# Attention followed by a state-space layer on one core: the convolution's first group projected in step 10 instead of 11, and the state's product behind the value matmuls of its step

## The reference

```python
# layer 0: attention over all 4096 pixels of an image
energy = q @ k                       # q, k: 32 channels
x1 = gamma * (softmax(energy) @ v) + x
# layer 1: on x1, per pixel in order
u = layernorm(x1)
z, xBC, dt = split(u @ in_w)         # 256, 512 and 4 columns
xBC = silu(causal_conv4(xBC) + b)    # 4 taps per channel
xs, Bm, Cm = split(xBC)              # 256, 128, 128
state = state * exp(dt*A) + (dt * xs) outer Bm
y = (state @ Cm + D * xs) * silu(z)
out = rmsnorm(y) @ out_w
result = x1 + out * sigmoid(mlp(mean(out)))
```

## Time and profile before

| | |
|---|---|
| median of 3 runs | 3118.52 us (3118.3 to 3119.95) |
| the profiled execution | 3119.77 us, span of its core 3117.6 us |
| PE busy | 2935.3 us, 94% |
| DVE, ACT, POOL busy | 66%, 62%, 64% |
| mean granted clock of PE | 0.978 |

### The profile page before, as it was taken

One profiled execution on the slowest core, in us unless ns is written; L12 is line 12 of the kernel. 1 busy time (PEld: TensorE's weight loads), 2 busy tenths in 40 slices (PEclk: granted clock), 3 DMA queues, 4 the chain that ended last, 5 costly groups with the idle time before them and its releaser, 6 DMA issues. The chain is left out here.

```text
span 3117.6 us, 62448 instructions
## 1 busy us (share of the span) xinstructions
PE 2935.3 (94%) x20696; PEld 2263.6 (73%) x20696; DVE 2047.6 (66%) x3577; ACT 1924.6 (62%) x3806; POOL 1991.1 (64%) x3087
## 2 busy tenths in 40 slices
PE   6889999999999999999999999999999999999974
PEld 3767777777767777777777777777777777777752
DVE  5556666666767666666676667676666667776553
ACT  2555666666656666666665666666666666666642
POOL 2446665677666676666676666576777666777753
PEclk9999999999999999999999999999999999999985
DMA  4111111111312112122221122122120111111021
GB/s 124 49 43 34 45 58 58 32 55 52 97 68 65 63 60 92 65 78 75 93 81 37 65 71 87 65 73 86 38 90 36 50 63 50 63 50 70 35 95 68
DMA packets 102512, 200.94 MB, mean 64 GB/s; under 512 B 18768, under 2 KB 41936, under 8 KB 97808
## 3 DMA queue, kind: packets, MB, share of 16 engines
q1 hardware_dynamic: 98192, 195.08, 18.4%
q10 hardware_dynamic: 4000, 1.86, 0.2%
HBM read 131.21 MB, written 64.75 MB: 63 GB/s over the span
## 5 line engine op out<-in xcount | busy, mean ns | idle before, releaser
L724 POOL TENSOR_TENSOR p_lo<-p,p_hi 128x512 f16<-128x512 f32 x1024 | 1201.4, 1181 | 747.7 <-ACT p_hi L887 598.5
L880 ACT ACTIVATE p<-p_et 128x512 f32<-128x512 f32 x1024 | 614.3, 600 | 603.3 <-PE p_et L1138 556.8
L1156 PE MATMUL acc<-v_hi,p_hi 128*128 128x257 f16 x4096 | 954.1, 273 | 2.6 <-DVE work L1456 1.5
L1158 PE MATMUL acc<-v_lo,p_hi 128*128 128x256 f16 x4096 | 952.2, 272 | 0.0
L1412 DVE TENSOR_REDUCE maxes<-p_mx 128x1 f32<-128x1024 f32 x508 | 619.8, 1220 | 321.2 <-PE p_mx L1117 321.1
L887 ACT ACTIVATE p_hi<-p 128x512 f16<-128x512 f32 x1024 | 646.2, 631 | 8.3
L1164 PE MATMUL acc<-v_hi,p_lo 128*128 128x257 f16 x4096 | 623.3, 274 | 16.4 <-POOL p_lo L724 16.4
L1156 PEld LDWEIGHTS acc<-v_hi,p_hi 128*128 128x128 f16 x4096 | 399.4, 98 | 128.8 <-issue 65.8
L1158 PEld LDWEIGHTS acc<-v_lo,p_hi 128*128 128x128 f16 x4096 | 400.5, 98 | 112.3 <-issue 43.3
L1164 PEld LDWEIGHTS acc<-v_hi,p_lo 128*128 128x128 f16 x4096 | 400.0, 98 | 69.9 <-POOL p_lo L724 17.6
L1138 PE MATMUL p_et<-qs,kst 98*128 98x256 f16 x2048 | 393.1, 273 | 3.6 <-ACT p L880 2.9
(11 more groups left out here) (214 smaller groups left out, 4160.3 us busy)
## 6 DMA issues: line engine op xcount, KB each, us to landing
work<-rows_d SPq DMA_DIRECT2D x32, 1024.0 KB, 4.9
xin<-in_x_dram SPq DMA_DIRECT2D x48, 512.0 KB, 5.0
xr<-in_x_dram SPq DMA_DIRECT2D x32, 512.0 KB, 3.7
x_d<-x1c SPq DMA_DIRECT2D x31, 512.0 KB, 3.0
og_d<-og SPq DMA_DIRECT2D x29, 512.0 KB, 2.7
mix_x<-x_d SPq DMA_DIRECT2D x25, 512.0 KB, 4.6
mix_o<-og_d SPq DMA_DIRECT2D x24, 512.0 KB, 5.5
out_dram<-mix_o SPq DMA_DIRECT2D x24, 512.0 KB, 3.0
```

The costliest lines, as they stand in the source:

```text
L724: e.tensor_tensor(p_lo[:, n % RING, :], p32[:, n % P32S, :], p_hi[:, n % RING, :], ALU.subtract).then_inc(lo_pool, 1)
L880: e.activation(p32[:, n % P32S, :], p_et[:, :], ACT.Exp).then_inc(exp_done, 1)
L1156: e.matmul(acc[:, t, 0:C + 1], p_hi[:, r, at:at + P], v_hi[:, 2 * k + kk, 0:C + 1], start=(k == 0 and kk == 0), stop=False)
L1158: e.matmul(acc[:, t, 0:C], p_hi[:, r, at:at + P], v_lo[:, 2 * k + kk, :], start=False, stop=False, skip_group_check=True)
```

## The change

Two things. `K_XBC[0]` goes from 11 to 10, which moves the first convolution group, with everything that follows it by a fixed number of steps, one step earlier on PE, ACT and DVE (in the last group all four). And `st` is no longer issued directly behind `y`, but behind `values` of the same step on PE; DVE's addition to the state (L1578) moves from the step of `y` to the one after it. No instruction is added or removed, and no DMA moves.

```diff
--- before.py
+++ after.py
@@ -49,7 +49,7 @@
 
 K_X1T, K_UT, K_DT, K_DAT, K_CUM, K_YT, K_OUT = 3, 9, 15, 25, 27, 30, 0
 K_U = (6, 7)
-K_XBC = (11, 16, 20, 26)
+K_XBC = (10, 16, 20, 26)
 K_Z = (10, 11, 13, 15)
 K_XSB = (26, 27, 28, 29)
 K_SRC = (1, 5, 9, 13)
@@ -143,7 +143,7 @@
             if K == K_CB[c]:
                 out += [("cb", Bk, c)]
             if K == K_Y[c]:
-                out += [("y", Bk, c), ("st", Bk, c)]
+                out += [("y", Bk, c)]
         if K == K_YT:
             out += [("yT", Bk, 0), ("yT", Bk, 1)]
     if s < G:
@@ -162,6 +162,9 @@
             out += [("se1", b, 0)]
         if K == 7:
             out += [("se2", b, 0)]
+    if 0 <= Bk < G and K in K_Y:
+
+        out += [("st", Bk, K_Y.index(K))]
     return out
 
 
@@ -1278,14 +1281,18 @@
                         max_pair(*of)
                 if s == 1 and K == 0:
                     e.wait_ge(w2_loaded, 16 * len(w_later))
-                for key in fills_at(s, K):
-                    fill(key)
+                fills = fills_at(s, K)
+                for key in fills:
+                    if key[0] != "st":
+                        fill(key)
                 if 0 <= s - 1 < G:
                     for m in range(CM):
                         if K == xbc_at(s - 1, m):
                             convolve(s - 1, m)
                 if s < G:
                     values(n)
+                if fills and fills[-1][0] == "st":
+                    fill(fills[-1])
 
             for j in range(NB):
                 qk(0, j)
@@ -1568,6 +1575,7 @@
                                                   cum16[:, c * NH:(c + 1) * NH].unsqueeze(2).to_broadcast([P, NH, HD]),
                                                   ALU.mult)
                         ins.then_inc(yt_ready, 1)
+                    if K == K_Y[c] + 1:
                         key = ("st", g, c)
                         e.wait_ge(filled, n_filled(key))
                         if first(g) and c == 0:
```

## The result

| | before | after |
|---|---|---|
| median of 16 runs each, side by side | 3118.95 us (3116.52 to 3121.6) | 3125.32 us (3122.21 to 3130.86) |
| the profiled execution's span | 3117.6 us | 3123.5 us |
| mean granted clock of PE | 0.978 | 0.979 |

The ratio is 1.0020, with a 95% interval of 1.0012 to 1.0027: slower by about 6 us, where 10 less were forecast. The page's busy times answer to the earlier trace rows; PE does the same work in less busy time and a longer span, so the 6 us are waits.

What follows compares the result with a forecast made beforehand. PE, busy 94% of the span, was taken as the bound, so its waits decide. Terms -28.7 + 1 + 23.9 - 3.3 - 3.9 + 1 = -10.0 against 3118.5 gave 3108.5, stated as 3108 us; range 3099 to 3119.

Steps and rivals of the forecast that it cites:

- step 8: `st` behind the values: PE's waits for `xw` and for the read-out of `yt` go, -28.7 us.
- step 9: The two `uT` wait for `qs` and `S`, 0 to 0.1 a slot, more in slots 12, 20, 28: +1 us.
- step 11: The second `z` waits for the first's read-out behind the moved convolution, 0.77 in 31 slots: +23.9 us.
- steps 12 to 14: DVE has two taps less ahead of the third `z`; 0.18 of waiting goes in 18 slots: -3.3 us.
- `qk` in steps 4 and 12: `qk` no longer waits for `yt`, 9 times 0.43: -3.9 us.
- tail: Last group's convolutions all move; two stand ahead of the second `z`'s tanh: +1 us, bounds -1 and +3.
- keep their order: 0: Convolutions two to four, the state from step 17 on, waits of steps 20 and 24: unchanged, 0 us.
- All signs that the prediction named for the profile: PE's waits: `xw` only in the tail, none for `yt`, about 30 of `z` for `zt`; clock as before.
- (a): POOL and DVE block each other, `st` waits again in step 8: +9, 3117.5 us; chance 0.2 with other partial losses.
- (b): Step 11's new wait lowers PE's clock: up to 3154 us; above 3122, chance 0.1 including a longer chain there.
- (c): The wait in step 11 is smaller as ACT and DVE overlap better: at half, 3096 us; chance 0.1.

Runs made afterwards that it cites:

- chunk 3 undone: The kernel after, with chunk 3 alone as before: in step 17 `st` directly behind `y` and `S` in that step; 3118.92 us, ratio 1.0002.
- e7: The kernel after, with one more POOL operation of 0.22 in the dt chain, ahead of the three `p_lo`; 3121.6 us, ratio 1.0006.

## Why the prediction was wrong, point by point

| step of the prediction | said | measured |
|---|---|---|
| step 8, 21 x 1.02 + 9 x 0.53 + 2.5 | -28.7 | -26.5 |
| step 9 | +1 | +4.1 |
| step 11, 31 x 0.77 (steps 10 and 11) | +23.9 | +28.8 |
| steps 12 to 14 (13 and 14 here) | -3.3 | -5.7 |
| `qk` in steps 4 and 12 | -3.9 | -9.8 |
| tail | +1 | +1.0 |
| "keep their order: 0" (16, 17, 20, 24, 26) | 0 | +12.0 |
| not spoken of (head, step 3) | 0 | +1.8 |
| sum | -10.0 | +5.9 |

(The parts measured make 5.7; 0.2 lies in steps that hardly changed.)

**The step that failed** is "Convolutions two to four, the state from step 17 on and the waits of steps 20 and 24 keep their order: 0". It cost 12.0, three quarters of the miss of 15.9. It has two faults. In step 17 the order is not kept: the change itself takes `S` out from ahead of the taps and of DVE's dt operations, and the prediction put that at nothing without a reason. And in steps 20 to 24, where the order is kept on every engine, the wait of step 24 grew all the same, by 10.9: order is not phase. The earlier trace rows left out the line of `mr` for `mparts`, 17.4 us in 26 waits, since the change did not touch it; it was the one to look at, for its operations of 0.16 that took 0.96 were already blocked once. The runs show the chain link by link: chunk 3 undone takes the loss away, the rows of step 17 and of POOL's `dtt` carry the 0.33 from `S` to the `p_lo`, 0.22 more on POOL takes most of the loss away, and `mparts` a step earlier all of it. The other terms missed by 2.2, 3.1, 4.9, -2.4 and -5.9, which is 1.9 in all: that the rest of the sum came so close is luck in part.

All signs that the prediction named for the profile came true: the waits that go, some 30 new ones of `z`, the clock, no `uT` waiting for `S`. None of them stood for the term put at nothing.

**Step 16**, +3.8 of the 12.0, is where a large part of the gain of step 14 goes: in 15 slots step 14 is 0.19 shorter and step 16 0.18 longer. PE waits there for DVE's `work` (L1463), 5.4 us in 20 waits where it was 1.5 in 3. In slot 5 one of DVE's dt operations is held until the end of the `p_lo` beside it in each of three kernels. That `p_lo` starts 0.85 (before), 0.67 (after) and 0.35 us (`z` read first) ahead of step 16, and `work` starts 1.92, 2.10 and 2.42 behind its start. These rows fit the same lock; no run moves this `p_lo` alone.

**Step 8 held.** The working of 1.02 and 0.53 from the earlier trace rows came out as 0.97 and 0.49. In slot 5, `y` takes 0.93 up to `mr`, where the prediction had 0.83 as up to `st`, and `st` behind the values takes 0.44 and not 0.48; that makes the 0.05. The unusual slot 8, for which 1.02 + 1.5 were added, gained 1.52 in step 8 and 0.80 in step 9.

**Step 11 was right in mechanism, off in size.** The chain of 2.26 was exact. The restart was taken as 0.05 from the earlier trace rows, where PE waits for `yt`; here PE starts 0.14 to 0.15 behind DVE's end, and the first `z` is 0.07 to 0.08 longer: 0.94 for 0.77, 5 us over 30 slots. The prediction's rows had both sizes: by the earlier trace rows, `xw` ends at 550.10 and `st` starts at 550.25, 0.15 behind it. Before the change all 22 waits for `xw` and all 26 for `mparts` restart in 0.14 to 0.15, all 19 of `mr` and `qk` for `yt` in 0.05. What makes the difference is not settled. The prediction counted 31 slots, and slot 1 has no wait; the 0.45 more of slot 31 makes up for half of it.

**Step 9** was taken as 0 to 0.1 a slot and is 0.14 in nearly all, with 0.37 to 0.49 in slots 12, 20 and 28. Its +1 was less than its own working: nearly all of step 8's gain in these three slots would be 2 by itself. **Steps 4 and 12** gained 0.42 to 0.43 per `qk`, as said, 0.39 in three slots more where another product (L1253) had waited for `yt`, and 0.057 in nearly every slot: `st` behind the values is 0.43 long up to the next product, where it was 0.49 ahead of them (0.48 in the prediction). Slot 17 gained 2.0 in its step 4, from a wait that was not worked out.

**Steps 13 and 14** gained the 0.18 that the prediction worked out, 0.19 here, in some 20 slots. In slots 10, 18 and 26, where it had 0, step 13 loses 1.07 each, as `xT` waits, and step 14 gains 1.52.

**The rivals.** (a), at 3117.5, named the right lock and was wrong on the place. In slot 5 `xw` ends 0.20 later against step 8 than before, well within the 0.79 to spare, and the scan of step 5 did meet `p_lo`, with 2.20 for 1.22, at no cost to PE:

```profile
545.62 2.20 DVE L1556 TENSOR_TENSOR_SCAN lt<-work,ident 128x512 f32<-128x512 f32 x1
```

(b) is refuted: 30 new waits of 0.7, one a slot, left the mean granted clock at 0.979. That frequent short idles cost throughput stands in the Trainium skill ("TensorE: Matmul & The Clock Gate") in the section "A second HAM failure mode: psum-queue depth-cycling", not in the one that the prediction names; no run here shows it. (c), the smaller wait, is refuted for the kernel as changed, and is what reading `z` first made of it.

## What to carry to other kernels

Where an engine's queue has short operations of two engines that can lock each other out, list them with their unblocked duration ahead of any change: one that takes six times its own time is a loss that a shift of 0.3 us far away can double or take away. An operation that leaves one queue shifts all that waits behind it, on other engines too. The blocked operation is better moved out of the other's long run (here worth 19 us) than tuned by phase. When a product is moved between two that share a bank, follow the read-out of the first through the order in which the reading engine takes its work; here a swap of two pieces on ACT was worth 23 us, more than the 10 of the half of the change that gained. And a change in two parts should be timed in its parts: one gained 10 us and the other lost 27, and together they looked like a small loss.

## What the runs showed of the hardware

A DVE operation on two columns, 0.16 us long, took 0.96 beside a POOL operation of 1.13. That was so for the form with two inputs from the core's memory (TENSOR_TENSOR) and for the one with a single input (TENSOR_SCALAR, fp32 to fp32: 0.97; fp32 to fp16: 1.17 in e7). The blocked ones of slot 7 end within 0.04 of the end of the POOL operation. PE restarts 0.14 to 0.15 behind the end of the operation that it waited for in the waits for `mparts`, `xw` and `z`, and 0.05 behind it in those for `yt`; the first fp32 product behind a wait of `z` was 0.07 to 0.08 longer than otherwise. And more work can be less time: one POOL operation of 0.22 a slot more took 8.3 us out of one step.
